# Attention scores on half-height tiles of the array, and a new order of the stages, in a fused three-layer kernel

## Chip, core and metric

One NeuronCore of a Trainium2 chip runs the whole program. The metric is the device time of one execution in microseconds (us), the median of several runs. The hardware profiler recorded one further execution, and all rows below come from it. TensorE is called PE here, its weight loads PEld, VectorE DVE, ScalarE ACT, GpSimd POOL, and SyncE, which issues most of the DMAs, SP.

## What is computed

For each of 64 images (cut from the reference):

```python
h = patchify(image) @ W.T + b + pos_emb          # 121 tokens of 192
h = concat([h, txt], axis=1)                     # 249 tokens
h = h + attn(layernorm(h))                       # 12 heads of 16 features
h = h + moe(layernorm(h))                        # 16 experts of 128, 4 chosen, and a shared one

# attn:
q, k, v = fq_act(x @ fq_weight(w_qkv).T + b_qkv)
a = fq_act(einsum('hnd,hmd->hnm', q, k) * 16 ** -0.5, s_attn)     # the score products
a = log_int_softmax(a, s_attn)                                   # integer exp, powers of two
o = fq_act(einsum('hnm,hmd->hnd', a, v))
return fq_act(o @ fq_weight(w_proj).T + b_proj)

# moe: softmax router, top 4 of 8 pairs, then top 4 experts, w_full[t, e]
y = sum_e w_full[:, e] * ((silu(x @ Wu[e] + bu[e]) * (x @ Wg[e] + bg[e])) @ Wd[e] + bd[e]) + shared(x)
```

## The kernel before, in words

All weights are loaded and converted once, and stay in SBUF. After that the kernel is a software pipeline over the images. One image is cut into 254 stages, each the work of one engine: `embed` (patches times weights, 14 recorded matmuls, L1075), `qk` and `v` (projections), six units k = 0..5 of attention (three groups of four heads, times two blocks of query tokens: the 128 text tokens for even k, the 121 patches for odd k), `project`, the router, and nine units k = 0..8 of experts (the shared one, then pairs).

The list `ORDER` (L304) writes out by hand one cycle of the pipeline: 254 triples of stage, shift and unit. In step j, each engine walks the list (`stages`, L359) and carries out those stages that are its own, for image j + shift. So image 0 is at `embed` while an older image is in its attention and a still older one in its experts. There are 69 steps for 64 images, since the shifts go down to -5. Each engine's instruction stream is thus in the list's order, and engines meet only at semaphores: a stage waits for its inputs, and for the buffer that it overwrites to be free. Where a stage stands in the list decides how early its engine comes to it.

The stages of an attention unit, with their engine and line, are: `score` (PE, L1111), `quant` (ACT, L598, the scores from PSUM to int8), `top` (DVE, L942, row maxima), `peak` (POOL, L516), `below` (ACT, L607), `quot` and `power` (DVE, L948, L953), `u` (PE, L1120 and L1121, a sum of two identity products into the same PSUM tile `pS`), `square` (ACT, L614), `expo` (DVE, L962), `sum` and `alpha` (DVE, L969, L974), `share` (ACT, L623), `low`, `grow`, `weigh` (DVE, L979, L983, L988), `turnp` (PE, L1132, eight transposes into `pX`), `copyp` (ACT, L632), and `value` (PE, L1142).

`score` holds four matmuls, one for each head of a group. The stationary operand is `qz`, queries in which each head's 16 features stand in a block of 32 partitions of their own and all other partitions are zero; the moving operand is `kb`, the keys of all four heads, 249 columns. All 128 rows of the array are used, and 96 of them multiply zeros. Heads 0 and 1 go to the first PSUM bank of `pS`, heads 2 and 3 to the second:

```python
for m in range(PER):
    a = mm(pS[0:n, m // 2, (m % 2) * TOKENS:(m % 2 + 1) * TOKENS],
           qz[:, g * PER + m, tcols[t]], kb[:, g, :], start=True, stop=True)
```

`value` holds eight matmuls whose outputs lie on 32 partitions each, so that they run on tiles of 32 columns of the array, four side by side; everything else in the loop uses the array whole. The experts' matmuls are `mmU` and `mmG` (L1183, ten of 250 columns per unit), `pick` (L1195, and for k = 1 six more, L1192) and `down` (L1209, float32). `chosen` (PE, L1167) transposes the routing weights, `copyw` (ACT, L668) copies them to SBUF as `w3T`, and `pick` waits for them.

`qz` is filled by DMAs on SP (`qzload`, L439) from what POOL has converted (`conv`, L497). SP also issues the image's 26 loads (`imgload`, L411), the text's and the stores.

Of the kernel before, what the change touches and what calls it, by code (L numbers as in the profile page):

```python
# [24 lines left out]
QUAD = 32  # L25
# [17 lines left out]
def fused_layer(nc, x, txt, tok_W, tok_b, pos_emb, w_qkv, b_qkv, w_proj, b_proj, sw_qkv, sw_proj,  # L43
# [14 lines left out]
    GROUPS, PER = HEADS // 4, 4  # L58
# [19 lines left out]
    with ctx:  # L78
# [63 lines left out]
        sq, y, v = ([cut(KEYS) for n in range(2)] for m in range(3))  # L142
# [147 lines left out]
        for t in range(2):  # L290
# [11 lines left out]
        block = ctx.enter_context(nc.Block())  # L302

        ORDER = [  # L304
            ("r_score", -4, -1), ("low", -3, 4), ("mmG", -5, 7), ("r_biased", -4, -1), ("weigh", -3, 3),
            ("qkq", -2, 5), ("turnp", -3, 3), ("alpha", -3, 5), ("conv", -2, 2), ("r_pairs", -4, -1),
            ("down", -5, 5), ("top", -2, 0), ("act", -5, 6), ("gate", -5, 7), ("grow", -3, 4),
            ("r_top_pairs", -4, -1), ("peak", -2, 0), ("score", -2, 1), ("share", -3, 5), ("silu", -5, 8),
            ("copyp", -3, 3), ("value", -3, 2), ("pick", -5, 7), ("outcast", -3, 0), ("quant", -2, 1),
            ("below", -2, 0), ("mmG", -5, 8), ("weigh", -3, 4), ("value", -3, 3), ("low", -3, 5),  # L310
            ("act", -5, 7), ("grow", -3, 5), ("top", -2, 1), ("turnp", -3, 4), ("down", -5, 6),
            ("r_take_pairs", -4, -1), ("gate", -5, 8), ("r_penalty", -4, -1), ("weigh", -3, 5), ("pick", -5, 8),
            ("outq", -3, 1), ("r_masked", -4, -1), ("act", -5, 8), ("copyp", -3, 4), ("outcast", -3, 1),
            ("score", -2, 2), ("down", -5, 7), ("value", -3, 4), ("quant", -2, 2), ("quot", -2, 0),
            ("mmU", -4, 0), ("top", -2, 2), ("peak", -2, 1), ("r_top", -4, -1), ("below", -2, 1),
            ("turnp", -3, 5), ("power", -2, 0), ("score", -2, 3), ("down", -5, 8), ("r_take", -4, -1),
            ("quot", -2, 1), ("mmG", -4, 0), ("copyp", -3, 5), ("value", -3, 5), ("result", -5, -1),
            ("power", -2, 1), ("quant", -2, 3), ("outq", -3, 2), ("qzload", -2, 2), ("v", -2, -1),
            ("silu", -4, 0), ("vq", -2, -1), ("u", -2, 0), ("outcast", -3, 2), ("r_weight", -4, -1),
            ("project", -3, -1), ("peak", -2, 2), ("square", -2, 0), ("top", -2, 3), ("prq", -3, -1),  # L320
            ("vconv", -2, -1), ("below", -2, 2), ("mmU", -4, 1), ("silu", -4, 1), ("peak", -2, 3),
            ("gate", -4, 0), ("residual", -3, -1), ("u", -2, 1), ("expo", -2, 0), ("quot", -2, 2),
            ("square", -2, 1), ("stats2", -3, -1), ("mean2", -3, -1), ("expo", -2, 1), ("below", -2, 3),
            ("embed", -1, -1), ("embed_h", -1, -1), ("score", -2, 4), ("mmG", -4, 1), ("sum", -2, 0),
# [5 lines left out]
            ("stats", -1, -1), ("mmG", -4, 2), ("u", -2, 2), ("power", -2, 2), ("mean", -1, -1),  # L330
            ("spread", -1, -1), ("turn2", -3, 0), ("copy2", -3, 0), ("mmU", -4, 3), ("square", -2, 2),
            ("store", -5, -1), ("act", -4, 1), ("turn2", -3, 1), ("quot", -2, 3), ("copy2", -3, 1),
            ("pick", -4, 2), ("down", -4, 1), ("gate", -4, 2), ("silu", -4, 3), ("low", -2, 0),
            ("norm", -1, -1), ("low", -2, 1), ("top", -2, 5), ("route", -3, -1), ("split", -1, -1),
            ("act", -4, 2), ("logit", -3, -1), ("lmax", -3, -1), ("expo", -2, 2), ("u", -2, 3), ("turn", -1, 0),
            ("power", -2, 3), ("mmG", -4, 3), ("below", -2, 4), ("copy", -1, 0), ("below_max", -3, -1),
            ("peak", -2, 5), ("square", -2, 3), ("sum", -2, 2), ("quot", -2, 4), ("gate", -4, 3),
            ("turn", -1, 1), ("alpha", -2, 2), ("grow", -2, 0), ("expo", -2, 3), ("copy", -1, 1),
            ("weigh", -2, 0), ("mmU", -4, 4), ("qk", -1, 0), ("u", -2, 4), ("mmG", -4, 4), ("power", -2, 4),
            ("pick", -4, 3), ("below", -2, 5), ("silu", -4, 4), ("gate", -4, 4), ("mmU", -4, 5),  # L340
            ("grow", -2, 1), ("act", -4, 3), ("qkq", -1, 0), ("gates", -3, -1), ("qk", -1, 1), ("sum", -2, 3),
            ("imgload", 0, -1), ("share", -2, 2), ("weigh", -2, 1), ("down", -4, 2), ("qk", -1, 2),
            ("mmG", -4, 5), ("qkq", -1, 1), ("silu", -4, 5), ("alpha", -2, 3), ("qkq", -1, 2), ("qk", -1, 3),
            ("r_ratio", -3, -1), ("mmU", -4, 6), ("qk", -1, 4), ("pick", -4, 4), ("quot", -2, 5),
            ("square", -2, 4), ("u", -2, 5), ("turnp", -2, 0), ("qkq", -1, 3), ("low", -2, 2), ("expo", -2, 4),
            ("gate", -4, 5), ("silu", -4, 6), ("mmU", -4, 7), ("qkq", -1, 4), ("share", -2, 3),
            ("r_exp", -3, -1), ("down", -4, 3), ("copyp", -2, 0), ("silu", -4, 7), ("sum", -2, 4),
            ("r_sum", -3, -1), ("act", -4, 4), ("square", -2, 5), ("r_inverse", -3, -1), ("grow", -2, 2),
            ("alpha", -2, 4), ("low", -2, 3), ("turnp", -2, 1), ("pick", -4, 5), ("down", -4, 4),
            ("conv", -1, 0), ("qzload", -1, 0), ("conv", -1, 1), ("power", -2, 5), ("weigh", -2, 2),  # L350
            ("expo", -2, 5), ("value", -2, 0), ("mmG", -4, 6), ("copyp", -2, 1), ("act", -4, 5), ("sum", -2, 5),
            ("value", -2, 1), ("gate", -4, 6), ("share", -2, 4), ("outq", -2, 0), ("turnp", -2, 2),
            ("copyp", -2, 2), ("pick", -4, 6), ("score", -1, 0), ("qzload", -1, 1), ("grow", -2, 3),
            ("mmU", -4, 8), ("qk", -1, 5), ("quant", -1, 0),
# [889 lines left out]
```

## Time and profile before

| | |
|---|---|
| runs | 3518.93 us, median of 3 (3518.01 to 3521.01) |
| profiled execution, its own time | 3518.62 us |
| its span, first to last instruction | 3516.8 us |
| around the span | 1.8 us |
| mean granted clock of TensorE | 0.989 of full speed |
| instructions | 98,077 |
| one cycle of the pipeline in the steady part | 52.2 us |

An engine is busy where at least one of its instructions is in flight. Instructions overlap their neighbours by some 0.07 us on DVE and 0.16 us on PE, so that the mean duration of one is longer than what it costs in a stream; the difference between two starts is the better price of a matmul.

### The profile page before, as it was taken

Reading aid. Unit: us, or ns where it says so; the run is one execution under the profiler, and the core shown is the slowest. Engines: PE = TensorE matmul, PEld = TensorE weight load, DVE = VectorE, ACT = ScalarE, POOL = GpSimd, SP = SyncE. Lnnn points to the kernel's source line nnn. Section 1 sums busy time; section 2 is a strip of 40 time slices with the busy share of each in tenths; the row PEclk is TensorE's granted clock in tenths of the full one; section 3 lists DMA queues with packets and bytes.
Section 4 is the critical chain, followed back from the end, with each engine's and each line's share of the span. In section 5 each row is a group of like instructions: output and inputs, shape, how many; then the busy total and the mean of one; then the engine's idle time right before and its main releaser. Section 6 shows DMA issues by size and latency. Waiting matters only on the chain.

```text
span 3516.8 us, 98077 instructions
## 1 busy us (share of the span) xinstructions
PE 3381.6 (96%) x30764; PEld 2898.6 (82%) x30764; DVE 3368.5 (96%) x10279; ACT 3153.6 (90%) x6228; POOL 806.2 (23%) x1647
## 2 busy tenths in 40 slices
PE   1589999999999999999999999999999999999999
PEld 1368888888888888888888888888888888888888
DVE  6699999999999999999999999999999999999995
ACT  2799999999999999999999999999999999999992
POOL 3222222222222222222221221222222222222210
PEclk9789999999999999999999999999999999999999
DMA  5101001000000000000000110100000000000000
GB/s 125 27 14 25 25 16 26 25 20 23 25 20 23 24 22 21 24 23 20 25 24 18 25 25 16 26 25 17 25 25 20 23 25 21 22 24 23 20 10 8
DMA packets 157123, 85.77 MB, mean 24 GB/s; under 512 B 51451, under 2 KB 154370, under 8 KB 156610
## 3 DMA queue, kind: packets, MB, share of 16 engines
q1 hardware_dynamic: 153692, 78.82, 9.0%
q8 instruction: 253, 4.15, 0.5%
q14 instruction: 260, 2.13, 0.2%
q10 hardware_dynamic: 2918, 0.67, 0.1%
HBM read 54.89 MB, written 12.24 MB: 19 GB/s over the span
## 4 chain that ended last, share of the span: by engine, by line
PE 92%; DVE 1%; issue 1%; ACT 0%; POOLq 0%; DVEq 0%; POOL 0%
PE pU L1183 33%; PE pY L1209 20%; PE pX L1075 5%; PE pX L1132 5%; PE pS L1120 4%; PE pS L1111 4%; PE pS L1121 4%; PE pX L1094 3%; PE pW L1195 3%; PE pO L1142 2%; PE pY L1192 1%; PE pX L1102 1%; PE pX L1088 1%; PE pX L1151 1%; PE pX L1082 1%
## 5 line engine op out<-in xcount | busy, mean ns | idle before, releaser
L1183 PE MATMUL pU<-x2T,UG 128*128 128x250 f16 x8704 | 1231.6, 270 | 1.0 <-ACT work L676 0.9
L1183 PEld LDWEIGHTS pU<-x2T,UG 128*128 128x128 f16 x8704 | 823.0, 97 | 108.7 <-ACT work L676 1.5
L1209 PE MATMUL pY<-WD,work 128*128 128x192 f32 (+1 forms) x4352 | 810.0, 328 | 0.0
L1209 PEld LDWEIGHTS pY<-WD,work 128*128 128x128 f32 (+1 forms) x4352 | 690.8, 187 | 3.9
L962 DVE SCALAR_TENSOR_TENSOR work<-work,cst 128x249 f32<-128x249 f32 (+1 forms) x1536 | 658.6, 484 | 8.4 <-issue 4.3
L623 ACT ACTIVATE work<-work,alpha 128x249 f32<-128x249 f32 (+1 forms) x1536 | 648.3, 509 | 15.2 <-DVE alpha L974 14.0
L607 ACT ACTIVATE work<-a,room 128x249 bf16<-128x249 int8 (+1 forms) x1536 | 648.3, 514 | 0.0
L1183 PE MATMUL pU<-x2T,UGB 67*128 67x250 f16 x2176 | 592.4, 272 | 0.0
L942 DVE TENSOR_REDUCE rmax<-a 128x4 f32<-128x996 int8 (+1 forms) x384 | 452.9, 1179 | 40.9 <-ACT a L598 40.9
L632 ACT ACTIVATE passing<-pX,cst 128x512 int16<-128x512 int16 (+3 forms) x768 | 480.8, 687 | 6.9 <-PE pX L1132 3.5
L598 ACT ACTIVATE a<-pS,cst 128x996 int8<-128x996 f32 (+1 forms) x384 | 421.4, 1097 | 70.3 <-PE pS L1111 70.1
L614 ACT ACTIVATE work<-pS,cst 128x996 f32<-128x996 f32 (+1 forms) x384 | 419.5, 1092 | 56.8 <-PE pS L1121 56.8
L983 DVE SCALAR_TENSOR_TENSOR work<-work 128x996 bf16<-128x996 bf16 (+1 forms) x384 | 453.1, 1180 | 0.1
L497 POOL TENSOR_SCALAR qb<-qk 128x249 bf16<-128x249 int8 x192 | 103.6, 540 | 1308.6 <-ACT qk L643 1307.5
L676 ACT ACTIVATE work<-pU 128x500 f32<-128x500 f32 (+1 forms) x576 | 326.0, 566 | 72.6 <-PE pU L1183 72.6
L1023 DVE TENSOR_TENSOR work<-pU,work 128x500 f32<-128x500 f32 x512 | 342.0, 668 | 17.3 <-PE pU L1183 17.1
L1028 DVE TENSOR_TENSOR work<-work,pW 128x500 f32<-128x500 f32 x512 | 339.2, 662 | 13.3 <-PE pW L1195 12.6
L1120 PE MATMUL pS<-work,ident 128*128 128x498 bf16 (+1 forms) x768 | 293.3, 382 | 7.7 <-ACT a L598 2.8
L1121 PE MATMUL pS<-work,identx 128*128 128x498 bf16 (+1 forms) x768 | 290.5, 378 | 0.0
L1111 PE MATMUL pS<-kb,qz 128*128 128x249 bf16 (+1 forms) x1536 | 232.6, 275 | 29.1 <-DMA qz<-qb 21.0
L979 DVE TENSOR_SCALAR work<-work 128x996 int16<-128x996 int16 (+1 forms) x384 | 255.2, 665 | 0.8 <-ACT work L623 0.7
L643 ACT ACTIVATE qk<-pX,qk_bias,qk_scale 128x249 int8<-128x249 f32 x384 | 219.1, 570 | 39.6 <-PE pX L1094 39.5
(209 smaller groups left out, 5337.5 us busy)
## 6 DMA issues: line engine op xcount, KB each, us to landing
img<-in_x_dram SPq DMA_DIRECT2D x896, 23.5 KB
img<-in_x_dram SPq DMA_DIRECT2D x768, 21.4 KB
qz<-qb SPq DMA_DIRECT2D x768, 15.6 KB, 1.8
h<-in_txt_dram SPq DMA_DIRECT2D x64, 96.0 KB, 2.0
out_dram<-yout SPq DMA_DIRECT2D x64, 96.0 KB
out_dram<-yout SPq DMA_DIRECT2D x64, 90.8 KB
WD<-in_L_ffn_Wd_dram SPq DMA_DIRECT2D x1, 1536.0 KB, 7.6
work<-in_L_ffn_Wu_dram SPq DMA_DIRECT2D x2, 512.0 KB, 6.6
```

The source lines that it names most:

```text
L598: sc_.activation(a8[b][0:n, :].rearrange("p (b c) -> p b c", b=2), pS[0:n, :, 0:2 * TOKENS], ACT.Copy, scale=cc(C_S, n)).then_inc(a_done, 1)
L607: a = sc_.activation(g16[b][0:n, c], a8[b][0:n, c], ACT.Relu, bias=room[b][0:n, m:m + 1])
L614: sc_.activation(sq[b][0:n, :].rearrange("p (b c) -> p b c", b=2), pS[0:n, :, 0:2 * TOKENS], ACT.Square, bias=cc(C_HL, n)).then_inc(sq_don ...
L623: a = sc_.activation(v[b][0:n, c], y[b][0:n, c], ACT.Copy, scale=alpha[b][0:n, m:m + 1])
L632: sc_.activation(probT[b][0:NTOK[t], :, t, 0:n].bitcast(I16), pt[0:NTOK[t], :, t, 0:n], ACT.Relu, bias=cc(C_OB, NTOK[t])).then_inc(prT_don ...
L942: ve.tensor_reduce(rmax[b][0:n, :], a8[b][0:n, :].rearrange("p (m c) -> p m c", m=PER), AX, ALU.max).then_inc(mx_done, 1)
L962: a = stt(out=y[b][0:n, c], in0=sq[b][0:n, c], scalar=cc(C_KC, n), in1=pw[b][0:n, c].bitcast(BF16), op0=ALU.add, op1=ALU.mult, accum_out=r ...
L983: stt(out=grown[b][0:n, :], in0=p16[b][0:n, :].bitcast(BF16), scalar=6.0, in1=v[b][0:n, :], op0=ALU.subtract, op1=ALU.mult).then_inc(gr_do ...
L1120: mm(pS[0:n, m, 0:2 * TOKENS], ident[0:n, 0:n], g16[b][0:n, c], start=True, stop=False)
L1121: a = mm(pS[0:n, m, 0:2 * TOKENS], identx[0:n, 0:n], q16[b][0:n, c], start=False, stop=True)
L1183: a = mm(pU[:, s, q * EVEN:(q + 1) * EVEN], weights, x2T[i % 2][0:w, m, 0:EVEN], start=m == 0, stop=m == BLOCKS - 1)
L1209: a = mm(pY[0:n, t * 256:t * 256 + D], (act_[k % 2] if k else up[0])[:, c:c + n], WD[:, e, :], start=k == 0 and t == 0, stop=e == E - 1, s ...
```

## The change

Two edits, and nothing else. The first lets each score matmul use 64 rows of the array only, those in which its head's features stand (rows 0 to 63 for heads 0 and 1, rows 64 to 127 for heads 2 and 3), and takes the heads in the order 0, 2, 1, 3, so that neighbours lie on different halves and write to different PSUM banks. The second replaces the whole list `ORDER` by another one of the same 254 stages. The cycle is cut at another place, so that most shifts read one higher; there are still 69 steps.

```diff
-            ("power", -2, 1), ("quant", -2, 3), ("outq", -3, 2), ("qzload", -2, 2), ("v", -2, -1),
-            ("silu", -4, 0), ("vq", -2, -1), ("u", -2, 0), ("outcast", -3, 2), ("r_weight", -4, -1),
-            ("project", -3, -1), ("peak", -2, 2), ("square", -2, 0), ("top", -2, 3), ("prq", -3, -1),
...
-            ("norm2", -3, -1), ("share", -2, 0), ("score", -2, 5), ("chosen", -4, -1), ("txtload", -1, -1),
-            ("top", -2, 4), ("copyw", -4, -1), ("mmU", -4, 2), ("quant", -2, 5), ("split2", -3, -1),
-            ("silu", -4, 2), ("peak", -2, 4), ("share", -2, 1), ("gate", -4, 1), ("pick", -4, 1),
...
+            ("u", -1, 0), ("gate", -3, 0), ("mmG", -3, 1), ("value", -2, 4), ("copyp", -2, 5), ("power", -1, 1),
+            ("value", -2, 5), ("top", -1, 2), ("result", -4, -1), ("peak", -1, 2), ("square", -1, 0),
+            ("top", -1, 3), ("v", -1, -1), ("silu", -3, 1), ("expo", -1, 0), ("r_weight", -3, -1),
+            ("outq", -2, 2), ("vq", -1, -1), ("u", -1, 1), ("outcast", -2, 0), ("sum", -1, 0), ("down", -3, 0),
+            ("r_part0", -3, -1), ("outcast", -2, 1), ("outcast", -2, 2), ("project", -2, -1), ("gate", -3, 1),
...
+            ("mean2", -2, -1), ("mmU", -3, 3), ("quant", -1, 4), ("quot", -1, 3), ("chosen", -3, -1),
+            ("spread2", -2, -1), ("sum", -1, 1), ("mmG", -3, 2), ("embed_h", 0, -1), ("share", -1, 0),
+            ("quant", -1, 5), ("low", -1, 0), ("silu", -3, 3), ("alpha", -1, 1), ("norm2", -2, -1),
+            ("u", -1, 2), ("stats", 0, -1), ("top", -1, 4), ("split2", -2, -1), ("copyw", -3, -1),
+            ("share", -1, 1), ("mean", 0, -1), ("gate", -3, 2), ("square", -1, 2), ("pick", -3, 1),
...
-                        for m in range(PER):
+                        for m in (0, 2, 1, 3):
+                            rows = slice(m // 2 * 2 * QUAD, (m // 2 + 1) * 2 * QUAD)
                             a = mm(pS[0:n, m // 2, (m % 2) * TOKENS:(m % 2 + 1) * TOKENS],
-                                   qz[:, g * PER + m, tcols[t]], kb[:, g, :], start=True, stop=True)
+                                   qz[rows, g * PER + m, tcols[t]], kb[rows, g, :], start=True, stop=True)
```

The stages of PE alone, where the text below speaks of them. Before: `... down8 mmG0 value5 v u0 project ...`, `... embed score4 mmG1 down0 score5 chosen mmU2 pick1 ...`, and the scores 0 to 3 stand ahead of `mmU8`, `value2`, `down7`, `down8`. After: `... down8 u0 mmG1 value4 value5 v u1 down0 project ...`, `... score4 embed score5 mmU3 chosen mmG2 u2 pick1 ...`, and the scores 0 to 3 stand ahead of `qk5`, `mmG7`, `down6`, `mmG0`. Also after, `value0` stands ahead of `down5`.

## Rows read from the trace of the kernel before

**Rows 1.** The page: span and busy time by engine.

```profile
span 3516.8 us, 98077 instructions
PE 3381.6 (96%) x30764; PEld 2898.6 (82%) x30764; DVE 3368.5 (96%) x10279; ACT 3153.6 (90%) x6228; POOL 806.2 (23%) x1647
```

**Rows 2.** Busy time by stretch: ten cycles of the steady part, the ramp, the end.

```profile
core 0: us, PE busy (x) PEld busy (x) DVE busy (x) ACT busy (x) POOL busy (x), PEclk, DMA share, GB/s
1022.00:1544.00 522.00, 520.99 (x4799) 449.82 (x4797) 515.92 (x1590) 487.97 (x970) 121.39 (x250) 1.00 0.09 23
...
54.90:263.80 208.90, 135.15 (x963) 97.80 (x964) 148.77 (x420) 149.69 (x289) 43.33 (x82) 0.82 0.08 18
3351.00:3517.00 166.00, 156.05 (x1403) 135.23 (x1402) 121.30 (x363) 94.50 (x187) 20.06 (x40) 1.00 0.03 7
```

**Rows 3.** The chain that ended last: two embeds three cycles apart (start us, us).

```profile
2983.07 3.33 PE pX L1075 x14
...
3139.62 3.33 PE pX L1075 x14
```

**Rows 4.** Timeline of PE around one value and one score unit.

```profile
1603.71 0.27 PE L1183 MATMUL pU<-x2T,UGB 67*128 67x250 f16 x1
1603.82 0.59 PE L1183 MATMUL pU<-x2T,UG 128*128 128x250 f16 x4
1604.25 0.27 PE L1183 MATMUL pU<-x2T,UGB 67*128 67x250 f16 x1
1604.45 0.30 PE L1142 MATMUL pO<-passing,vb 128*32 128x121 bf16 x8
1604.68 0.62 PE L1132 MATMUL pX<-ident,passing 128*128 128x128 bf16 x8
...
1605.36 0.59 PE L1111 MATMUL pS<-kb,qz 128*128 128x249 bf16 x4
1605.79 0.48 PE L1183 MATMUL pU<-x2T,UG 128*128 128x250 f16 x3
```

**Rows 5.** Timeline of the setup: transposes of 128 rows, then of 64 rows.

```profile
53.05 0.71 ACT L577 ACTIVATE wT<-pU 128x384 f16<-128x384 f16 x2 [0.21 <-PE pU L1049]
...
53.60 0.24 PEld L1049 LDWEIGHTS pU<-ident,p_int 128*128 128x128 bf16 x3 [0.47 <-ACT wT L577]
...
54.03 0.18 PEld L1049 LDWEIGHTS pU<-ident,p_int 64*128 64x128 bf16 x3 [0.20 <-issue]
```

**Rows 6.** Waits in 40 cycles of the steady part: us in total, times, longest.

```profile
PEld pO L1142 <- issue: 40.9, 200, 0.2
...
PEld pY L1192 <- issue: 12.6, 40, 0.6
DVE v L937 <- PE pX L1104: 11.9, 38, 0.4
```

**Rows 7.** Groups by form over the whole span: weight loads.

```profile
L1209 PEld LDWEIGHTS pY<-WD,work 128*128 128x128 f32 x2304 | 375.2, 190 | 3.9
...
L1111 PEld LDWEIGHTS pS<-kb,qz 128*121 128x121 bf16 x768 | 89.2, 137 | 10.2 <-issue 6.8
...
L1111 PEld LDWEIGHTS pS<-kb,qz 128*128 128x128 bf16 x768 | 80.4, 105 | 36.5 <-DMA qz<-qb 21.5 <-issue 3.7
```

**Rows 8.** Timeline from a `chosen` to the next `pick` of unit 1.

```profile
1629.47 1.68 ACT L623 ACTIVATE work<-work,alpha 128x249 f32<-128x249 f32 x4 [0.15 <-DVE alpha L974]
...
1630.18 0.28 PE L1167 MATMUL pX<-ident,w 128*96 128x128 bf16 x2
...
1631.06 0.36 ACT L668 ACTIVATE w3T<-pX 96x256 bf16<-96x256 bf16 x1
...
1631.33 1.07 ACT L598 ACTIVATE a<-pS,cst 121x996 int8<-121x996 f32 x1
...
1631.54 0.46 PEld L1192 LDWEIGHTS pY<-BD,w3T 96*128 96x128 bf16 x6 [0.29 <-issue]
```

**Rows 9.** The page's groups: the silu stages on ACT.

```profile
L676 ACT ACTIVATE work<-pU 128x500 f32<-128x500 f32 (+1 forms) x576 | 326.0, 566 | 72.6 <-PE pU L1183 72.6
```

More of the change, by code:

```diff
@@ L304, in fused_layer @@
         ORDER = [
[L305 to L314, printed above, removed]
@@ L320, in fused_layer @@
-            ("project", -3, -1), ("peak", -2, 2), ("square", -2, 0), ("top", -2, 3), ("prq", -3, -1),
[L321 to L324, printed above, removed]
@@ L330, in fused_layer @@
[L330 to L334, printed above, removed]
@@ L335, in fused_layer @@
[L335 to L354, printed above, removed]
+            ("low", -2, 2), ("down", -4, 2), ("weigh", -2, 0), ("below_max", -3, -1), ("qkq", -1, 2),
@@ new lines, in fused_layer @@
+            ("square", -2, 4), ("alpha", -2, 3), ("imgload", 0, -1), ("qk", -1, 3), ("expo", -2, 4),
+            ("power", -2, 5), ("sum", -2, 4), ("pick", -4, 4), ("qkq", -1, 3), ("mmU", -4, 6), ("qk", -1, 4),
+            ("gates", -3, -1), ("act", -4, 4), ("silu", -4, 6), ("vconv", -2, -1), ("gate", -4, 5),
+            ("down", -4, 3), ("share", -2, 3), ("alpha", -2, 4), ("u", -2, 5), ("grow", -2, 2), ("qkq", -1, 4),
+            ("square", -2, 5), ("pick", -4, 5), ("turnp", -2, 0), ("copyp", -2, 0), ("r_ratio", -3, -1),
@@ new lines, in fused_layer @@
+            ("mmU", -4, 7), ("act", -4, 5), ("share", -2, 4), ("mmG", -4, 6), ("r_exp", -3, -1),
+            ("pick", -4, 6), ("weigh", -2, 1), ("conv", -1, 0), ("qzload", -1, 0), ("turnp", -2, 1),
+            ("copyp", -2, 1), ("down", -4, 4), ("low", -2, 3), ("expo", -2, 5), ("score", -1, 0),
+            ("gate", -4, 6), ("sum", -2, 5), ("grow", -2, 3), ("alpha", -2, 5), ("weigh", -2, 2),
+            ("r_sum", -3, -1), ("silu", -4, 7), ("qk", -1, 5), ("value", -2, 0), ("low", -2, 4),
+            ("down", -4, 5), ("quant", -1, 0), ("qkq", -1, 5), ("share", -2, 5), ("score", -1, 1),
@@ new lines, in fused_layer @@
+            ("quant", -1, 1), ("conv", -1, 1), ("qzload", -1, 1), ("top", -1, 0), ("r_inverse", -3, -1),
+            ("mmG", -4, 7), ("turnp", -2, 2), ("act", -4, 6), ("value", -2, 1), ("r_score", -3, -1),
+            ("gate", -4, 7), ("mmU", -4, 8), ("r_biased", -3, -1), ("pick", -4, 7), ("weigh", -2, 3),
+            ("copyp", -2, 2), ("mmG", -4, 8), ("silu", -4, 8), ("outq", -2, 0), ("conv", -1, 2),
+            ("grow", -2, 4), ("turnp", -2, 3), ("score", -1, 2), ("low", -2, 5), ("down", -4, 6),
@@ new lines, in fused_layer @@
+            ("store", -5, -1), ("r_pairs", -3, -1), ("mmU", -3, 0), ("value", -2, 2), ("weigh", -2, 4),
+            ("act", -4, 7), ("pick", -4, 8), ("peak", -1, 0), ("top", -1, 1), ("below", -1, 0),
+            ("turnp", -2, 4), ("gate", -4, 8), ("r_top_pairs", -3, -1), ("down", -4, 7), ("score", -1, 3),
+            ("copyp", -2, 3), ("mmG", -3, 0), ("grow", -2, 5), ("qzload", -1, 2), ("r_take_pairs", -3, -1),
+            ("peak", -1, 1), ("quant", -1, 2), ("value", -2, 3), ("silu", -3, 0), ("act", -4, 8),
@@ new lines, in fused_layer @@
+            ("u", -1, 2), ("stats", 0, -1), ("top", -1, 4), ("split2", -2, -1), ("copyw", -3, -1),
+            ("share", -1, 1), ("mean", 0, -1), ("gate", -3, 2), ("square", -1, 2), ("pick", -3, 1),
+            ("spread", 0, -1), ("power", -1, 3), ("peak", -1, 4), ("act", -3, 1), ("turn2", -2, 0),
+            ("norm", 0, -1), ("mmU", -3, 4), ("split", 0, -1), ("copy2", -2, 0), ("pick", -3, 2),
+            ("silu", -3, 4), ("top", -1, 5), ("turn2", -2, 1), ("copy2", -2, 1), ("peak", -1, 5),
@@ new lines, in fused_layer @@
+            ("mmG", -3, 3), ("u", -1, 3), ("grow", -1, 0), ("below", -1, 4), ("gate", -3, 3), ("turn", 0, 0),
+            ("copy", 0, 0), ("mmU", -3, 5), ("turn", 0, 1), ("square", -1, 3), ("act", -3, 2), ("expo", -1, 2),
+            ("quot", -1, 4), ("mmG", -3, 4), ("route", -2, -1), ("down", -3, 1), ("copy", 0, 1), ("sum", -1, 2),
+            ("logit", -2, -1), ("qk", 0, 0), ("low", -1, 1), ("gate", -3, 4), ("u", -1, 4), ("expo", -1, 3),
+            ("qk", 0, 1), ("pick", -3, 3), ("alpha", -1, 2), ("lmax", -2, -1), ("mmG", -3, 5), ("silu", -3, 5),
@@ L355, in fused_layer @@
+            ("below", -1, 5), ("quot", -1, 5), ("power", -1, 4), ("sum", -1, 3), ("qkq", 0, 0), ("qk", 0, 2),
+            ("grow", -1, 1), ("qkq", 0, 1), ("share", -1, 2), ("act", -3, 3),
         ]
```

12 lines of the change are left out of this document (7 added, 5 removed).

## The prediction

> **What bounds the kernel now.** I read the page first: PE and DVE are both busy 96% of the span, ACT 90% [rows 1], so the average does not say which one decides. The stretches do. In the steady part PE is busy 520.99 of 522 us, DVE 515.92, ACT 487.97 [rows 2]: per cycle of 52.2 us that is 52.1 for PE, 51.6 for DVE, 48.8 for ACT. The chain that ended last goes through PE's matmuls, and its embeds are (3139.62 - 2983.07) / 3 = 52.18 us apart [rows 3]. So the cycle is PE's stream, one matmul after the other at the full granted clock, and DVE stands 0.6 us behind it. That second number caps what a lighter PE can bring: no DVE instruction is changed, so the cycle cannot fall much below 51.6 us, a gain of 0.6 us per cycle whatever the matmuls do. The bound holds from about 250 us to about 3420 us, 61 cycles; in the ramp PE is busy 135.15 of 208.9 us and part of it at the low clock, and at the end the stages thin out (156.05 of 166 us) [rows 2]. One tenth of a us per cycle is therefore worth 6 us. What a measurement of this kernel can tell from no change is about 0.2%, 7 us, or 0.115 us per cycle.
>
> **The halves, priced.** A score unit now costs four matmuls, from 1605.36 to 1605.79, 0.43 us [rows 4], six units per cycle. Two pairs, each side by side, would cost 2 x 0.107 = 0.21 us, if nothing else came with it. Something else does, and the kernel has a sample of it: `value`, whose matmuls use tiles of 32 columns, four abreast. Read the starts, since ends are modelled. A 250-column matmul streams 0.11 us (1603.71 to 1603.82). The last one before the value unit starts at 1604.25, the value unit at 1604.45: 0.20 us, 0.09 more than its stream. From there to the first whole-array matmul is 0.23 us (1604.68), for two rounds of 121 columns, 0.05 each: 0.12 more [rows 4]. Together 0.21 us for going into the tiled form and out of it again. The weight loads, which elsewhere run one matmul ahead, stop in front of each value unit with nothing to wait for: 200 times in 40 cycles, 0.20 us each [rows 6], the sixth unit being booked to its data.
>
> Does a tile of half the rows pay the same as a tile of a quarter of the columns? The steady part has no such matmul, but the setup has: transposes of 64 rows behind transposes of 128. The ACT move that frees their bank ends at 53.76, and yet their weight load starts only at 54.03, idle for 0.20 us under "issue", while the 128-row load before it starts at 53.60 with ACT as its releaser [rows 5]. So going to half the rows also empties the array first. The way back is hidden behind ACT there.
>
> The Trainium skill has a rule for each side. "TensorEngine Tiling (Array Packing)", Key Properties, says that changing the tiling mode drains the TensorE; the trace agrees, by the 0.21 us above. "TensorE: Matmul & The Clock Gate", Part 3, says that tiles on different rows start within 4 ns of each other, and gives 3.07 times for four of them; by that alone the score units would fall by half, as in the first rival below. No row here shows two half-row tiles abreast.
>
> The unit then costs 0.09 in, 0.21 for two pairs, 0.01 offset within a pair, 0.10 out: 0.41 to 0.42 against 0.43. I take **-0.01 us each, -0.06 per cycle**. The bounds: without any switch -0.21 x 6 = -1.3 per cycle; with the switch and no overlap at all within the pairs +0.21 x 6 = +1.3. I stay at the value, since its row is the nearest, and since two rows show the switch. Two smaller doubts push upward. The weights of 121 columns load in 137 ns against 105 [rows 7]; if two halves load one after the other, each unit grows by some 0.05. And in the new list score 2 and value 0 stand ahead of `down`, score 4 ahead of `embed`, whose float32 weights load in 190 ns and more [rows 7]; out of a value unit today the next matmuls are never float32. If all of a load showed, this would be 3 x 0.1 = 0.3 per cycle. I take nothing for it, since in rows 4 the matmul starts with its own load, and keep it for the range.
>
> **The order.** Its 254 stages hold the same instructions, so it can only remove or add waits and switches. On PE, `value` 4 and 5 become neighbours, with no whole-array matmul between: one way in and out less, **-0.20 us per cycle**. This is sure as far as the list goes, and its price is the 0.21 above less the offset of the second group. The only true wait of PE in the steady part is at `pick` 1, which needs `w3T`: its weight load stops 12.6 / 40 = 0.31 us per cycle [rows 6], of which some 0.2 are lost by the stream. After the change `mmG` 2 and `u` 2 stand between `chosen` and `pick` 1 where `mmU` 2 alone stood, so PE brings 0.86 us more of cover (`u` is four matmuls of 498 columns, each twice the 0.107 of 249). But `copyw` on ACT has moved behind `quant` 5 and `silu` 3, so the outcome is open, and I take 0, with -0.2 as the lower bound and the second rival as the upper.
>
> The other moved stages get nothing. On SP, `imgload` (26 issues) and `txtload` stand about as far ahead of `embed` as before, 32 against 31.5 us of matmuls for the image; the cover is more than half a cycle, and SP is seldom busy. `qzload` 0 stands 8 us of matmuls behind `qk` 3 and 2 us ahead of `score` 0, about as before; if that cover went, PE would stand for the DMA and the POOL cast, a few tenths. On POOL the three `outcast` now follow each other just ahead of `project`, but `v`, `u` 1 and `down` 0 lie between the last `value` and `project`, 2.2 us against 1.5 before. On DVE, `vq` waits 11.9 / 40 = 0.30 us per cycle for PE [rows 6] and does so again, since `v` again stands right ahead of it. Ramp and end: from `embed` to `result` it is 3.9 cycles in both lists; I take 0 and +-6 us.
>
> **The sum.** -0.06 - 0.20 = -0.26 us per cycle, to 51.9, which still lies above DVE's 51.6. Times 61: -16 us. Against the profiled execution, 3518.6, that gives 3502.7; the median of the runs is 0.3 above it: **3503 us**.
>
> **Rivals.**
> *The pairs cost half and nothing more.* The row switch is cheap, as the way back is seen in no row. PE falls by 1.3 + 0.2 to 50.7, and DVE becomes the bound: 51.6 busy, with the remaining waits 51.7. That is -0.5 x 61 = -30 us, 3488. For it: the products touch other rows and other banks. Against it: rows 4 and 5.
> *The wait at `pick` 1 grows (slower).* Today the copy of `w3T` starts at 1631.06, when `share` ends, 0.88 behind `chosen`, and PE stands 0.2 for it [rows 8]. If ACT comes to it in the new list only after `quant` 5 (1.07 as recorded [rows 8], 0.97 in a stream) and `silu` 3 (0.57 at most [rows 9]), it is 1.5 later, against the 0.86 of new cover. The wait grows by 0.65, and the cycle by 0.65 - 0.26 = +0.39: +24 us, 3543. It decides from a growth of 0.26 on. Against it: ACT has 3.4 us of idle time per cycle and may come earlier.
> *No difference.* The switches eat all of the pairs' gain and half a tenth more, and a new wait of a tenth eats the rest: 3512 to 3526. For it: two engines this full answer to any shift with small waits.
> *The pairs do not overlap, and the change does not do what it says.* The switches are paid on top: +1.3 - 0.2 = +1.1, +65 us, 3584. Only if both halves share one path for their weights or data; value's columns do not.
>
> **How the numbers follow.** Forecast 0.38, cheap halves 0.17, no difference 0.21, grown wait (or another of its size) 0.19, no overlap 0.05. Faster by over 0.2% is 0.55, within it 0.21, slower 0.24. The forecast's own range is 3490 to 3511. The range that holds 8 in 10 takes in the cheap halves down to 3480 and the grown wait up to 3543, and leaves out the last rival and the tails.
>
> **What would show it.** By steps: a score unit takes 0.41 to 0.43 us from its first start to that of the next stage plus the gap before it, with the weight loads idle by 0.2 us ahead of each; two score matmuls start within 0.02 us of each other; 160 rather than 200 idle stops in front of `value`; embeds 51.9 us apart. Wrong, if the stops ahead of score are missing (then DVE's busy share goes to 99% or more and embeds come 51.7 apart), if L1192 or any other PE line waits over 0.3 us per cycle, or if PE's busy share falls below 99% in the steady part while DVE's does not rise.

## The result, and the profile after

The changed kernel takes 3621.61 us (median of 3 runs, 3621.53 to 3622.49) against 3518.93 before: a ratio of 1.0291, with a 95% interval of 1.0268 to 1.0315. It is 103 us slower where 16 us of gain were forecast, and it lies far outside the range.

The page of the changed kernel, which answers to [rows 1]:

```profile
span 3620.7 us, 98077 instructions
PE 3412.5 (94%) x30764; PEld 2805.5 (77%) x30764; DVE 3387.4 (94%) x10279; ACT 3181.0 (88%) x6228; POOL 925.1 (26%) x1647
```

The stretches, ten old cycles long, to set beside [rows 2] (columns as there):

```profile
1022.00:1544.00 522.00, 510.14 (x4616) 421.61 (x4614) 503.11 (x1547) 476.82 (x941) 137.84 (x243) 1.00 0.09 22
```

PE idles 12 us of 522 where it idled 1, and DVE 19 where it idled 6. In this stretch one engine alone is busier: POOL, 137.84 us against 121.39, and over the span 925 against 806 with the same 1647 instructions. That is the first hint. The granted clock is 1.00 in both stretches, so it has no part in the longer cycle.

The chain that ended last, beside [rows 3]: its shares, then two embeds twelve cycles apart.

```profile
PE 87%; POOL 4%; issue 1%; DVE 0%; ACT 0%; POOLq 0%; DVEq 0%; ACTq 0%
...
2698.37 3.62 PE pX L1074 x14
3345.59 3.62 PE pX L1074 x14
```

POOL was at 0% and is at 4%, and the cycle is (3345.59 - 2698.37) / 12 = 53.94 us, 1.7 more than 52.2. In this kernel the lines from `split` on stand one lower: `embed` is L1074, `turn` L1081, the subtraction L533, `grow` L982.

The same chain in one cycle, where it leaves PE:

```profile
1629.13 0.18 PE pX L1087 x3
...
1629.59 0.52 POOL xs L496
...
1630.28 2.00 POOL xs L533
1632.28 0.05 issue
1632.33 0.34 PE pX L1081 x3
```

The timeline of that place, with POOL, DVE and PE side by side:

```profile
1630.28 1.99 POOL L533 TENSOR_TENSOR xs<-xn,xs 128x384 f16<-128x384 f32 x1 [0.18 <-POOL xs L496]
1630.31 1.19 DVE L982 SCALAR_TENSOR_TENSOR work<-work 128x996 bf16<-128x996 bf16 x1
...
1630.97 0.37 PE L1121 MATMUL pS<-work,identx 121*121 121x498 bf16 x1
1631.42 0.67 DVE L1022 TENSOR_TENSOR work<-pU,work 128x500 f32<-128x500 f32 x1
...
1632.33 0.34 PE L1081 MATMUL pX<-ident,xs 128*128 128x128 f16 x3 [0.98 <-POOL xs L533]
```

PE stands 0.98 us ahead of `turn`, which transposes the normalized tokens for the next image's projections, because POOL's `split` is late: in every cycle of the steady part `turn` starts 0.056 to 0.058 us behind the end of the subtraction. And `split` is late because its subtraction takes 1.99 us. The groups of POOL say that it always does, first in the changed kernel:

```profile
L533 POOL TENSOR_TENSOR xs<-xn,xs 128x384 f16<-128x384 f32 x64 | 126.3, 1973 | 11.7 <-POOL xs L496 11.7
```

and then the same instruction in the kernel before:

```profile
L534 POOL TENSOR_TENSOR xs<-xn,xs 128x384 f16<-128x384 f32 x64 | 58.7, 917 | 11.7 <-POOL xs L497 11.7
```

The operands are the same, and the mean is 1.06 us longer. What differs is DVE's instruction beside it. Before, a reduction and a multiplication with one input in PSUM ran there; now it is `grow`, 1.1 us to the next start, both inputs in SBUF.

The score units came out close to the price that was worked out. The timeline around one of 121 columns, whose weight loads (PEld) and matmuls (PE) answer to [rows 4]:

```profile
1662.51 0.19 PEld L1111 LDWEIGHTS pS<-kb,qz 64*121 64x121 bf16 x4 [0.23 <-issue]
1662.51 0.43 PE L1111 MATMUL pS<-kb,qz 64*121 64x249 bf16 x4
...
1662.87 0.33 PEld L1183 LDWEIGHTS pU<-x2T,UG 128*128 128x128 f16 x4 [0.17 <-issue]
1662.87 0.60 PE L1183 MATMUL pU<-x2T,UG 128*128 128x250 f16 x4
```

The weight loads stop ahead of the unit and behind it. Start to start it is 0.36 us, plus 0.09 for the way in, 0.45 in all, against 0.43 before. Over the steady part, by the starts in the trace: the two matmuls of a pair start 0.003 us apart; the second pair starts 0.114 behind the last start of the first with weights of 128 columns and 0.153 with 121; the next whole-array matmul starts 0.20 behind the last one. That makes 0.41 and 0.45 us per unit, three of each per cycle.

### The profile page after: what moved, and what is told of

It reads as the page before. It is cut to its first block, busy times and chain, and to the rows that moved or that the text cites. A ratio compares the mean times of both kernels' runs of the same rounds, so it can differ in the third digit from the quotient of the medians.

```text
span 3620.7 us, 98077 instructions
## 1 busy us (share of the span) xinstructions
PE 3412.5 (94%) x30764; PEld 2805.5 (77%) x30764; DVE 3387.4 (94%) x10279; ACT 3181.0 (88%) x6228; POOL 925.1 (26%) x1647
## 4 chain that ended last, share of the span: by engine, by line
PE 87%; POOL 4%; issue 1%; DVE 0%; ACT 0%; POOLq 0%; DVEq 0%; ACTq 0%
PE pU L1183 31%; PE pY L1209 21%; PE pX L1074 6%; PE pX L1132 5%; PE pX L1093 4%; PE pS L1120 4%; PE pS L1121 4%; PE pS L1111 3%; POOL xs L533 3%; PE pW L1195 3%; PE pO L1142 2%; PE pX L1151 1%; PE pX L1101 1%; POOL xs L496 1%; PE pX L1081 1%
## 5 line engine op out<-in xcount | busy, mean ns | idle before, releaser
L1183 PEld LDWEIGHTS pU<-x2T,UG 128*128 128x128 f16 x8704 | 805.0, 97 | 136.1 <-issue 32.0
L1209 PE MATMUL pY<-WD,work 128*128 128x192 f32 (+1 forms) x4352 | 830.5, 333 | 0.0
L961 DVE SCALAR_TENSOR_TENSOR work<-work,cst 128x249 f32<-128x249 f32 (+1 forms) x1536 | 677.4, 496 | 26.6 <-issue 24.7
L982 DVE SCALAR_TENSOR_TENSOR work<-work 128x996 bf16<-128x996 bf16 (+1 forms) x384 | 453.7, 1181 | 0.0
L496 POOL TENSOR_SCALAR qb<-qk 128x249 bf16<-128x249 int8 x192 | 134.0, 698 | 1109.2 <-ACT qk L642 1098.2
L515 POOL TENSOR_SCALAR room<-rmax,cst 128x4 f32<-128x4 f32 (+1 forms) x384 | 124.8, 325 | 830.1 <-DVE rmax L941 823.6
```

Of the source, the lines that this page charges most:

```text
L961: a = stt(out=y[b][0:n, c], in0=sq[b][0:n, c], scalar=cc(C_KC, n), in1=pw[b][0:n, c].bitcast(BF16), op0=ALU.add, op1=ALU.mult, accum_out=r ...
L982: stt(out=grown[b][0:n, :], in0=p16[b][0:n, :].bitcast(BF16), scalar=6.0, in1=v[b][0:n, :], op0=ALU.subtract, op1=ALU.mult).then_inc(gr_do ...
L1183: a = mm(pU[:, s, q * EVEN:(q + 1) * EVEN], weights, x2T[i % 2][0:w, m, 0:EVEN], start=m == 0, stop=m == BLOCKS - 1)
L1209: a = mm(pY[0:n, t * 256:t * 256 + D], (act_[k % 2] if k else up[0])[:, c:c + n], WD[:, e, :], start=k == 0 and t == 0, stop=e == E - 1, s ...
```

## The experiments

Eleven kernels ran. Three theories stood against each other: the halves cost the time (B); the new order costs it through POOL's late subtraction, one wait with one cause (A); the new order stands so close everywhere that another wait takes over whatever is done about the first (D). Some expectations also name C, that the halves help and the order hides it, and split A into A1, POOL stands still while `grow` runs, and A2, POOL is late for its place in its own queue.

**Halves alone.** The kernel before, with the diff's second hunk only.

> The old order of the stages, with the score products on half-height tiles. Theory A (the new order costs, the halves are about even): the trace of the changed kernel shows a score unit of 128 columns of weights at 0.41 us, way in and out included, and one of 121 columns at 0.45, against 0.43 before, so +0.03 us per cycle over six units; two of the units stand ahead of float32 matmuls here, +0.06 each, and one stands right ahead of a value unit, which saves one way in, -0.1. Sum +0.05 per cycle, times 61: 3522 us, within 3510 to 3540, embeds 52.2 us apart. Theory B (the halves are what costs the 103 us): 3600 or more. Theory C (the halves help and the order hides it): 3490.

Measured: 3527.49 us (ratio 1.0024, 1.0015 to 1.0033). B falls, and so does C. The halves cost 9 us in the old order, 0.13 us per cycle, where A named 0.05. The score units gain 0.52 us per cycle by the starts, their way in included; against it the two `down` groups that stand behind a score unit take 0.38 us more, way out included, and all other stages together 0.28 more.

**Order alone.** The kernel before, with the new `ORDER` only.

> The new order of the stages, with the score products on the whole array as before. Theory A: the wait of PE at L1081 (turn 0, behind POOL's subtraction of xs) stays, about 1.0 us per cycle, and the time stays near the changed kernel's: minus 0.03 per cycle for the units, minus 0.3 for float32 matmuls behind a tile switch (the embed group takes 3.33 us again, not 3.62), so 3621 - 0.33 x 62 = 3601 us, within 3590 to 3622. Theory B: the time falls to 3519 or below.

Measured: 3608.02 us (1.0254, 1.0238 to 1.0269), with L533 at 1975 ns and PE's wait still there. The order costs 89 us, and the halves 14 on top of it. The embed group, which stands right behind score 4 in the new order, takes 3.43 to 3.44 us here, 3.62 with the halves, and 3.33 in the old order.

**`grow` moved away, in the new order.** `("grow", -1, 0)` goes behind `("act", -3, 2)`:

```diff
-            ("mmG", -3, 3), ("u", -1, 3), ("grow", -1, 0), ("below", -1, 4), ("gate", -3, 3), ("turn", 0, 0),
-            ("copy", 0, 0), ("mmU", -3, 5), ("turn", 0, 1), ("square", -1, 3), ("act", -3, 2), ("expo", -1, 2),
+            ("mmG", -3, 3), ("u", -1, 3), ("below", -1, 4), ("gate", -3, 3), ("turn", 0, 0),
+            ("copy", 0, 0), ("mmU", -3, 5), ("turn", 0, 1), ("square", -1, 3), ("act", -3, 2), ("grow", -1, 0), ("expo", -1, 2),
```

> The changed kernel, with one DVE stage moved: grow 0 (L982, both inputs in SBUF, 1.1 us) goes from ahead of gate 3 to behind act 2, so that POOL's subtraction of xs (L533) runs beside gate and act, which read one input from PSUM. Theory A1 (POOL stands still while grow runs): the mean of L533 falls from 1973 ns to 920, PE's wait at L1081 from 1.0 us per cycle to below 0.1, embeds come 52.9 us apart, and the time is 3621 - 1.0 x 62 = 3559 us, within 3545 to 3575. Theory A2 (POOL is late for another reason, its place in its own queue): L533 stays at 1973 ns and the time within 10 us of 3621. Theory B (halves): no effect either.

Measured: 3591.87 us (1.0207, 1.019 to 1.0224). The instruction is fast again:

```profile
L533 POOL TENSOR_TENSOR xs<-xn,xs 128x384 f16<-128x384 f32 x64 | 60.8, 949 | 11.8 <-POOL xs L496 11.8
```

So the slow subtraction was `grow`'s doing, and POOL's place in its queue is ruled out. But only 30 of the 62 us that A1 named came back, outside its range for the time. By the starts of the matmuls over 30 cycles, PE's interval ahead of `turn` is 1.07 us per cycle shorter than in the changed kernel, and of that 0.51 are lost again ahead of the `qk` stages and 0.22 ahead of `pick`, while 0.18 are won ahead of `turnp`. The timeline of this run shows the new wait, at a `qk` stage further on:

```profile
1678.51 0.17 DVE L973 RECIPROCAL alpha<-rsumc 128x4 f32<-128x4 f32 x1
...
1678.71 1.68 ACT L622 ACTIVATE work<-work,alpha 128x249 f32<-128x249 f32 x4 [0.38 <-DVE alpha L973]
...
1680.30 0.54 ACT L642 ACTIVATE qk<-pX,qk_bias,qk_scale 128x249 int8<-128x249 f32 x1
...
1680.99 0.48 PE L1093 MATMUL pX<-xT,wT 128*128 128x249 f16 x3 [0.34 <-ACT qk L642]
```

`alpha` comes later behind the moved `grow`, ACT takes `share` before `qkq`, and PE waits for `qkq` to empty the tile `pX`.

**`grow` put beside `split`, in the old order.** This was to add the suspected cost alone to the kernel before: `("grow", -2, 0)` goes from behind `("alpha", -2, 2)` to ahead of `("top", -2, 5)`.

```diff
-            ("norm", -1, -1), ("low", -2, 1), ("top", -2, 5), ("route", -3, -1), ("split", -1, -1),
+            ("norm", -1, -1), ("low", -2, 1), ("grow", -2, 0), ("top", -2, 5), ("route", -3, -1), ("split", -1, -1),
...
-            ("turn", -1, 1), ("alpha", -2, 2), ("grow", -2, 0), ("expo", -2, 3), ("copy", -1, 1),
+            ("turn", -1, 1), ("alpha", -2, 2), ("expo", -2, 3), ("copy", -1, 1),
```

> The kernel before, whole products, old order, with the same DVE stage put where it meets POOL's subtraction: grow 0 stands ahead of top 5 (a reduction with one input), which then comes 1.1 us later. Theory A1: in the old order L534 takes 917 ns; now it meets the last 0.46 us of grow and takes about 1380 ns (up to 1990 if it starts together with it), ending up to 0.5 to 1.1 us later, while PE reaches its turn stage only 0.57 us after the subtraction's end: PE waits 0 to 0.5 us per cycle, 3519 to 3550 us. Theory A2: L534 stays at 917 ns and the time at 3519 within 7 us, but for what the later top 5 does.

Measured: 3578.78 us (1.017, 1.0155 to 1.0185), 60 us slower, beyond A1's range. By the starts of the matmuls all of it, 1.0 us per cycle, lies ahead of `turn` 0. The timeline there:

```profile
1611.06 1.77 POOL L497 TENSOR_SCALAR xs<-xn 128x384 f16<-128x384 f32 x1 [1.49 <-DVE xn L932]
...
1611.28 1.18 DVE L983 SCALAR_TENSOR_TENSOR work<-work 128x996 bf16<-128x996 bf16 x1
...
1613.02 0.91 POOL L534 TENSOR_TENSOR xs<-xn,xs 128x384 f16<-128x384 f32 x1 [0.18 <-POOL xs L497]
...
1614.07 0.18 DVE L1003 SCALAR_TENSOR_TENSOR logit<-pX,gb 128x32 f32<-128x32 f32 x1
...
1614.39 0.33 PE L1082 MATMUL pX<-ident,xs 128*128 128x128 f16 x3 [0.82 <-DVE logit L1003]
```

`grow` met the cast and not the subtraction: the cast took 1.77 us where it takes 0.67 or 0.51, so it lost about the length of `grow`. This repeats the effect on POOL in the other order. It does not price it, because PE's wait has a second cause here, and that one ends last. `turn` writes the tile `pX` behind `route`, so it also waits until DVE's `logit` has read `route`'s result, and `grow` now stands on DVE ahead of `top` 5, `act` 2 and `logit`, which all come later by its 1.1 us. In all cycles of the steady part `turn` 0 starts 0.146 us behind the end of `logit`, to a nanosecond, and 0.45 to 0.46 us behind the end of the subtraction, where in the changed kernel it was 0.057. A subtraction that ended earlier would not have let `turn` start earlier: the 60 us come by way of `logit`, a rival that the expectation did not have. What the run does show is how little room this order has: one DVE stage of 1.1 us, moved past eleven others of DVE, costs more than half of what the whole change does.

**The subtraction left out.** The changed kernel, with nothing moved:

```diff
-                        nc_.tensor_tensor(xs[:, :, D:2 * D], xn[:], xs[:, :, 0:D],
-                                          ALU.subtract).then_inc(xs_done[0], 1)
+                        nc_.memset(xs[:, :, D:2 * D], 0.0).then_inc(xs_done[0], 1)
```

> The changed kernel with no list altered; in split (POOL) the subtraction xn - xs, which gives the low part of the float16 split, is left out and its half of the tile set to zero by a memset, which reads nothing. It ends some 1.5 us earlier, beside the same grow on DVE. So PE's wait at L1081 goes with nothing else moved. Theory A: minus 1.05 us per cycle, embeds 52.9 apart, 3556 us, within 3548 to 3575, and what is left over the kernel before, 0.6 us per cycle, lies in float32 matmuls behind a tile switch and small waits. Theory D: at most half is kept, above 3590.

Measured: 3569.56 us (1.0143, 1.0128 to 1.0158). The memset took 418 ns beside the same `grow`, and PE waits at `turn` no more. This prices the wait at 52 us, net of what comes in its place; A had said 65, and its range just holds, while D's is missed by 20 us. By the starts of the matmuls the interval ahead of `turn` is 1.15 us per cycle shorter, and 0.29 of that are lost again ahead of `qk` and 0.21 ahead of `pick`, while 0.17 are won ahead of `turnp`. The edit takes away the whole subtraction and not only its delay; with the delay alone gone (`grow` moved) it was 1.07 us shorter, so nearly all of the wait was the delay.

**Both taken away.** The same edit with whole products.

```diff
-                        for m in (0, 2, 1, 3):
-                            rows = slice(m // 2 * 2 * QUAD, (m // 2 + 1) * 2 * QUAD)
+                        for m in range(PER):
...
-                                   qz[rows, g * PER + m, tcols[t]], kb[rows, g, :], start=True, stop=True)
+                                   qz[:, g * PER + m, tcols[t]], kb[:, g, :], start=True, stop=True)
```

> The new order with whole score products and the subtraction xn - xs left out (a memset in its place): both suspected costs taken away together. Each alone gave 3621 to 3608 (whole products, 13 us) and 3621 to 3570 (subtraction, 52 us). If they add, 3556 us, within 3550 to 3562, and the rest of the 102 us, 37 us, belongs to other waits of the new order, under the kernel before's 0.2 us per cycle each. If they hide each other: 3569 or more.

Measured: 3554.99 us (1.01, 1.0084 to 1.0117). They add: 14 or 15 us for the halves and 52 or 53 for the wait, whichever goes first. There remain 36 us over the kernel before, some 0.6 us per cycle by the embeds. In that run's waits, for 40 cycles:

```profile
PEld pX L1092 <- issue: 31.9, 80, 0.5
...
PEld pW L1193 <- DVE work L1026: 19.2, 46, 0.7
...
PEld pX L1149 <- issue: 13.5, 39, 0.7
```

These are the `qk` stages, `pick` behind DVE's `act`, and `project`. The first two have no line of this size in the steady part of the kernel before; `project` had one of 16.1 us there. By the starts of the matmuls the intervals ahead of `qk` are 0.54 us per cycle longer than in the kernel before and those ahead of `pick` 0.27, while those ahead of `value` are 0.36 shorter. Such an interval also holds the stream of the matmul in front of it, which is another one in the new order, so this says where the 36 us lie and is no price of a single wait.

**Can PE cover the wait?** Two kernels left DVE alone and moved PE's list. In the first, `mmU` 5 went ahead of `turn` 0 and `mmG` 4 ahead of `turn` 1:

```diff
-            ("mmG", -3, 3), ("u", -1, 3), ("grow", -1, 0), ("below", -1, 4), ("gate", -3, 3), ("turn", 0, 0),
-            ("copy", 0, 0), ("mmU", -3, 5), ("turn", 0, 1), ("square", -1, 3), ("act", -3, 2), ("expo", -1, 2),
+            ("mmG", -3, 3), ("u", -1, 3), ("grow", -1, 0), ("below", -1, 4), ("gate", -3, 3), ("mmU", -3, 5),
+            ("turn", 0, 0), ("copy", 0, 0), ("square", -1, 3), ("act", -3, 2), ("expo", -1, 2),
...
+            ("quot", -1, 4), ("mmG", -3, 4), ("turn", 0, 1), ("route", -2, -1), ("down", -3, 1), ("copy", 0, 1), ("sum", -1, 2),
```

> The changed kernel, with PE's list alone altered: mmU 5 goes ahead of turn 0, and mmG 4 ahead of turn 1, so that PE has 1.07 us of expert products to do while POOL subtracts xs beside grow. DVE's list is untouched. Theory A (a wait that other work of PE can cover): L533 stays at 1973 ns, PE's wait at L1081 falls from 1.0 to about 0.1 us per cycle, and most of that is kept, 3621 - 0.9 x 62 = 3565 us, within 3555 to 3580. Theory D (moving grow later gave back half because a loop through DVE and ACT stands right behind the wait in this order, whatever is done about POOL): only about half is kept here too, 3590 us, and the new wait is at L1093, the qk stage.

Measured: 3615.82 us (1.0273, 1.0258 to 1.0288), 6 us gained. The wait at `turn` went, and one of nearly its size appeared at `route`, which I had put right behind `turn` 1 while ACT still had to empty `pX`:

```profile
PEld pX L1160 <- issue: 36.5, 39, 0.9
```

That was a fault of the edit, so the second kernel also put `down` 1 between `turn` 1 and `route`, and `pick` 3 between `route` and `qk` 0.

```diff
-            ("quot", -1, 4), ("mmG", -3, 4), ("turn", 0, 1), ("route", -2, -1), ("down", -3, 1), ("copy", 0, 1), ("sum", -1, 2),
-            ("logit", -2, -1), ("qk", 0, 0), ("low", -1, 1), ("gate", -3, 4), ("u", -1, 4), ("expo", -1, 3),
-            ("qk", 0, 1), ("pick", -3, 3), ("alpha", -1, 2), ("lmax", -2, -1), ("mmG", -3, 5), ("silu", -3, 5),
+            ("quot", -1, 4), ("mmG", -3, 4), ("turn", 0, 1), ("down", -3, 1), ("route", -2, -1), ("copy", 0, 1), ("sum", -1, 2),
+            ("logit", -2, -1), ("pick", -3, 3), ("qk", 0, 0), ("low", -1, 1), ("gate", -3, 4), ("u", -1, 4), ("expo", -1, 3),
+            ("qk", 0, 1), ("alpha", -1, 2), ("lmax", -2, -1), ("mmG", -3, 5), ("silu", -3, 5),
```

> The changed kernel, PE's list alone altered again: mmU 5 ahead of turn 0, mmG 4 ahead of turn 1, and now down 1 between turn 1 and route, pick 3 between route and qk 0, so that no user of the tile pX stands right behind the one before it. In the run without the last two moves PE waited 0.95 us per cycle ahead of route for ACT's copy, in place of the 1.1 at turn 0. Theory A (each wait can be covered by moving PE work): 0.85 us per cycle is kept, embeds 53.1 us apart, 3621 - 0.85 x 62 = 3568 us, within 3555 to 3585. Theory D (in this order the engines stand so close to each other that a loop of nearly the same length takes over): above 3595.

Measured: 3625.88 us (1.0304, 1.0289 to 1.0319), 4 us slower than the changed kernel. `turn` and `route` no longer wait, but `qk` does:

```profile
PEld pX L1093 <- issue: 71.7, 156, 0.8
```

Covering the wait with other PE work did not help in either form. The likely reason is that what is late is data: copies, six `qk` stages and ACT's `qkq` follow `turn` one by one through the single tile `pX`. No run separates this from the other moves.

**A second move on ACT.** The run with `grow` moved, and `share` 2 put behind `qkq` 2, into the next cycle.

```diff
-            ("square", -2, 4), ("alpha", -2, 3),
+            ("share", -2, 2), ("square", -2, 4), ("alpha", -2, 3),
...
-            ("grow", -1, 1), ("qkq", 0, 1), ("share", -1, 2), ("act", -3, 3),
+            ("grow", -1, 1), ("qkq", 0, 1), ("act", -3, 3),
```

> The kernel with grow 0 moved behind act 2, and on ACT share 2 moved behind qkq 2, into the next cycle. In the run without this second move PE waits at L1093 for qkq, since ACT does share 2 first, and share 2 waits for alpha 2, which stands behind grow 0 on DVE. Theory A (each of these is one wait with one cause): that wait, some 0.5 us per cycle, goes too, embeds come 52.9 us apart: 3560 us, within 3550 to 3575. Theory D (a loop of the whole order): the time stays within 8 us of 3592.

Measured: 3619.37 us (1.0283, 1.0268 to 1.0299), 28 us worse than without it. DVE's `low` then waits for `share` (10.0 us in 40 cycles), and PE's `pick` for DVE (38.9 us on its weight loads). A's reading of that wait as one with one cause is wrong; D predicted no gain, but not this loss.

**The price of a switch, alone.** The kernel before, with `value` 0 put ahead of `value` 1 and `value` 2 ahead of `value` 3:

```diff
-            ("copyp", -3, 3), ("value", -3, 2), ("pick", -5, 7), ("outcast", -3, 0), ("quant", -2, 1),
-            ("below", -2, 0), ("mmG", -5, 8), ("weigh", -3, 4), ("value", -3, 3), ("low", -3, 5),
+            ("copyp", -3, 3), ("pick", -5, 7), ("outcast", -3, 0), ("quant", -2, 1),
+            ("below", -2, 0), ("mmG", -5, 8), ("weigh", -3, 4), ("value", -3, 2), ("value", -3, 3), ("low", -3, 5),
...
-            ("expo", -2, 5), ("value", -2, 0), ("mmG", -4, 6), ("copyp", -2, 1), ("act", -4, 5), ("sum", -2, 5),
+            ("expo", -2, 5), ("mmG", -4, 6), ("copyp", -2, 1), ("value", -2, 0), ("act", -4, 5), ("sum", -2, 5),
```

> The kernel before with whole score products, and value 0 moved right ahead of value 1 and value 2 right ahead of value 3, behind the expert products that stood between. Nothing else. By the price of a tile switch, 0.09 in and 0.11 out, two fewer of each are 0.4 us per cycle: PE's stream goes to 51.8 us, still above DVE's 51.6, and the time to 3519 - 0.4 x 61 = 3495 us, within 3488 to 3508. If the gaps around value are no cost of a switch but waits for ACT's copies, the time stays at 3519 within 6 us, or rises, since the copies come no earlier.

Measured: 3498.57 us (0.994, 0.9924 to 0.9957), 20.7 us under the 3519.27 of the kernel before beside it, within the expectation, and faster than both kernels. The same with values 4 and 5 paired as well:

```diff
-            ("score", -2, 2), ("down", -5, 7), ("value", -3, 4), ("quant", -2, 2), ("quot", -2, 0),
+            ("score", -2, 2), ("down", -5, 7), ("quant", -2, 2), ("quot", -2, 0),
...
-            ("quot", -2, 1), ("mmG", -4, 0), ("copyp", -3, 5), ("value", -3, 5), ("result", -5, -1),
+            ("quot", -2, 1), ("mmG", -4, 0), ("copyp", -3, 5), ("value", -3, 4), ("value", -3, 5), ("result", -5, -1),
```

> The old order with whole products and values 0 and 1, 2 and 3, and now 4 and 5 side by side. With the first two pairs the cycle is 51.88 us, PE is busy 99.8% and DVE 99.5% of the steady part, 51.6 us per cycle. If PE alone decided, a third switch saved would bring 0.2 per cycle, 3487 us. With DVE at 51.6 at least, no more than 0.2 can come, and I expect 0 to 0.15: 3490 to 3499 us.

Measured: 3495.02 us (0.993, 0.9914 to 0.9947), the best version found. The third pair brought only 3.6 us, less than the 7 us that the prediction set as the least that can be told, though the runs of the two kernels do not overlap; it saves as much of switching as each of the others. Its stretch of ten old cycles:

```profile
1022.00:1544.00 522.00, 520.94 (x4854) 454.67 (x4852) 519.31 (x1606) 490.43 (x979) 121.59 (x250) 1.00 0.09 23
```

DVE is busy 519.31 of 522 us, 99.5%, where it was at 515.92 [rows 2]. That leaves the third pair little to gain, and the waits show DVE taking over: `turnp` now stops for DVE's `weigh`, in a line that the kernel with two pairs does not have.

```profile
PEld pX L1132 <- DVE passing L988: 9.7, 40, 0.3
```

## Why the prediction was wrong

**What bounds the kernel** was right: PE's stream decides in the old order, and DVE follows at 51.6 us per cycle. The pairing runs stopped at 51.8 to 51.9.

**The halves** were right in kind and off in size. The switch into half the rows costs what it costs into a quarter of the columns, and the two matmuls of a pair do run side by side, so the drain eats the gain. The forecast was -0.06 per cycle; measured are +0.13 in the old order and +0.22 (14 us over 62 cycles) in the new. Units of 128 columns gave the expected 0.41 us, units of 121 columns 0.45. The two doubts that I priced at nothing, the one on the weights and the one on float32, are both real: the second pair of 121-column weights starts 0.153 and not 0.107 behind the first, and float32 work behind a score unit pays more, 0.19 for `embed`.

**The paired values** were right: 0.20 per switch was forecast, and two of them gave 20.7 us, 0.34 per cycle, with DVE's bound already felt.

In the changed kernel the weight loads stop 153 times in 39 cycles in front of `value`, four per cycle where it was five.

**The wait at `pick` 1** went the good way. L1192 has no line among the waits of the changed kernel, so the second rival, the slower one, had the right sign and named the wrong place. That this was "the only true wait of PE" before was a misreading: the same 40 cycles have a larger one, at `project` for POOL's `outcast`.

```profile
PEld pX L1151 <- POOL ob L497: 16.1, 40, 0.5
```

**The step that failed** is "the other moved stages get nothing", and under it the premise that the order "can only remove or add waits and switches". I took every duration from the old trace as a property of the instruction. For POOL it depends on the neighbour too: the subtraction's 0.92 us was true beside a reduction, and 1.99 is true beside `grow`. Of POOL's stages I had looked at the three `outcast` and at none of `split`, and `turn` had stood only 0.57 us behind the subtraction's end (the timeline of the kernel before has the subtraction from 1636.98 to 1637.90, and `turn` at 1638.47). The Trainium skill, in "SBUF — State Buffer", Who interferes with whom, says that a DVE instruction with two SBUF inputs contends with a GpSimd instruction that reads SBUF, and one that only writes it does not. The runs agree on both: the subtraction went from 0.92 to 1.99 us, and the memset was over after 0.418 us, while the same `grow` was still in flight. It should have been a rival with a price of its own.

**The account of the 103 us**: 52 for the wait behind the slow subtraction, 14 for the halves, and 36 for other waits of the new order. The 52 and the 14 are shown by taking them away, singly and together. The 36 lie mostly ahead of `qk` and `pick`, but no run took them away one by one, and whether a list near this one is free of them stays open. Theory A holds for the cause of the wait at `turn`, though not as "one wait with one cause": with it gone, 0.5 of its 1.15 us per cycle came back ahead of `qk` and `pick`. D holds for the repair: of four attempts to move stages around the wait, one brought 30 us of the 62 that were named, one 6, and two made it worse than the kernel or the run they started from. Theory B is refuted.

## What to carry to other kernels

Before a hand-written order is changed, list for each GpSimd instruction on a dependent path what VectorE does at that moment, in the old order and the new; durations of GpSimd that are read from one order need not hold in another. When one stage is moved as a test, look at which wait ends last behind it: the move of `grow` in the old order delayed `split` as intended, and the time came from `logit`. A tile of the array that is smaller than the whole paid 0.2 us here for the way in and out, so price it against the group between the switches (here 0.43 us, of which half was to be saved), and put groups of one tile shape side by side first: that gave 0.7% here with three stages moved. When two engines are both near full, test an order on the chip in single moves, since a wait removed from one loop returned in the next.

## What the runs showed of the hardware

Beside `grow`, a VectorE instruction of 1.18 us with two inputs in SBUF, a GpSimd instruction that reads SBUF was longer by nearly all of `grow`: the subtraction took 1.99 for 0.92 us, the cast 1.77 for 0.67, and `grow` its usual 1.18. Two inputs in SBUF are not needed for some delay: that cast takes 0.51 us beside a reduction and 0.67 when it begins during `low`, a 16-bit instruction with one input.

It is not always GpSimd that loses. Where its cast is clearly in front and nothing holds it, VectorE does. In the changed kernel a cast for `v` starts 0.10 us ahead of the first instruction of `expo`, which also has two inputs in SBUF:

```profile
1038.86 0.51 POOL L509 TENSOR_SCALAR vb<-v 128x384 bf16<-128x384 int8 x1
1038.95 0.68 DVE L961 SCALAR_TENSOR_TENSOR work<-work,cst 128x249 f32<-128x249 f32 x1
...
1039.56 0.47 DVE L961 SCALAR_TENSOR_TENSOR work<-work,cst 128x249 f32<-128x249 f32 x1
```

The cast keeps its 0.51 us, and `expo` takes 0.68 for 0.47, so in every cycle. In the run with `grow` moved, the same cast starts 0.36 us ahead of another `grow` and also keeps its 0.51. The recorded starts do not always tell who is first: the subtraction is recorded 0.03 us ahead of `grow` and loses, and the cast in the old order begins while `low` is still in flight.

Going from whole-array matmuls to tiles of 64 rows or of 32 columns cost about the same here, 0.09 us in and 0.10 us out where no float32 matmul follows, and matmuls on the two halves of the rows start 0.003 us apart. The duration recorded for a matmul shows little of this (276 ns in the new form with 128 columns of weights for 274 before, 296 for 275 with 121); starts and the idle time of the weight loads do.
